# One copy of V, overwritten in place, and eight probability buffers in the first attention of a two-layer block

## The reference

```python
H, D = 16, 64
q = (x @ Wq).reshape(B, S, H, D).transpose(0, 2, 1, 3)
k = (c @ Wk).reshape(B, N, D, H).transpose(0, 3, 2, 1)
v = (c @ Wv).reshape(B, N, D, H).transpose(0, 3, 1, 2)
mask = jnp.all(c == 0, axis=-1)[:, None, None, :]
scores = jnp.einsum('bhsd,bhdn->bhsn', q, k) * scale
att = jax.nn.softmax(jnp.where(mask, -jnp.inf, scores), axis=-1)
out = jnp.einsum('bhsn,bhnd->bhsd', att, v)
x = x + out.transpose(0, 2, 1, 3).reshape(B, S, H * D) @ Wo
```

## Time and profile before

| what | value |
|---|---|
| median of 3 runs | 2121.53 us (2121.21 to 2129.98) |
| the profiled execution | 2127.05 us |
| its span, first to last instruction | 2125.3 us |
| PE, DVE, ACT, POOL busy | 1982.3, 1693.7, 1065.4, 1161.7 us |
| `subtract` L741 | 832 times, 685 ns |
| row maximum L682 | 1024 times, 589 ns |
| copy of a V chunk by ACT L556 | 208 times, 592 ns |
| denominator sum on POOL L374 | 352 and 32 times, 2.4 us |

### The profile page before, as it was taken

One profiled execution on the slowest core, in us unless ns is written; L12 is line 12 of the kernel. 1 busy time (PEld: TensorE's weight loads), 2 busy tenths in 40 slices (PEclk: granted clock), 3 DMA queues, 4 the chain that ended last, 5 costly groups with the idle time before them and its releaser, 6 DMA issues. The chain is left out here.

```text
span 2125.3 us, 35171 instructions
## 1 busy us (share of the span) xinstructions
PE 1982.3 (93%) x10757; PEld 1451.8 (68%) x10757; DVE 1693.7 (80%) x4048; ACT 1065.4 (50%) x1493; POOL 1161.7 (55%) x624
## 2 busy tenths in 40 slices
PE   5999999999999999999999999999966899779995
PEld 4677777777677777767777777777645688557774
DVE  7898888888887888888888888888647777757765
ACT  3445445453545545453545545454534799644442
POOL 0275756657575655757575666657764445314340
PEclk9899999999999999999999999999986999879997
DMA  3000000000000000000000000000000212112210
GB/s 95 1 1 17 1 4 17 1 1 4 18 1 4 2 16 1 4 18 1 1 4 17 1 4 1 1 1 1 1 6 16 91 60 75 38 49 63 74 35 24
DMA packets 54855, 40.84 MB, mean 19 GB/s; under 512 B 2500, under 2 KB 51596, under 8 KB 53644
## 3 DMA queue, kind: packets, MB, share of 16 engines
q1 hardware_dynamic: 54668, 38.57, 6.1%
HBM read 37.45 MB, written 1.11 MB: 18 GB/s over the span
## 5 line engine op out<-in xcount | busy, mean ns | idle before, releaser
L374 POOL TENSOR_TENSOR a_den<-a_den,a_probs 128x1024 f32<-128x1024 f32 x352 | 844.3, 2402 | 332.2 <-ACT a_probs L572 331.8
L572 ACT ACTIVATE a_probs<-a_probs,a_mask_col 128x1024 f32<-128x1024 f32 x416 | 478.8, 1151 | 571.8 <-DVE a_probs L741 571.7
L741 DVE TENSOR_TENSOR a_probs<-a_scores,a_shift 128x512 f32<-128x512 f32 x832 | 565.0, 685 | 160.1 <-PE a_scores L399 138.8
L682 DVE CUSTOM_DVE_ANT_0 a_work<-a_work,a_mask_row 128x400 f32<-128x400 f32 (+1 forms) x1024 | 571.7, 589 | 47.7 <-PE a_work L431 47.3
L479 PE MATMUL a_pv<-a_probs,a_V 128*64 128x256 f32 x3328 | 405.2, 385 | 1.0 <-ACT a_probs L572 0.9
L397 PE MATMUL a_scores<-a_Q_hi,a_cT_hi 128*128 128x512 f32 x832 | 345.7, 415 | 6.4 <-DVE a_probs L741 4.6
L431 PE MATMUL a_work<-a_cT_hi,a_Q_hi 128*128 128x400 f32 (+1 forms) x1024 | 328.0, 369 | 2.4
L398 PE MATMUL a_scores<-a_Q_lo,a_cT_hi 128*128 128x512 f32 x832 | 328.1, 394 | 0.0
L399 PE MATMUL a_scores<-a_Q_hi,a_cT_lo 128*128 128x512 f32 x832 | 326.6, 393 | 0.0
L479 PEld LDWEIGHTS a_pv<-a_probs,a_V 128*64 128x64 f32 x3328 | 220.5, 136 | 150.3 <-issue 39.1
L431 PEld LDWEIGHTS a_work<-a_cT_hi,a_Q_hi 128*128 128x128 f32 x1024 | 193.7, 190 | 98.3 <-issue 43.1
(11 more groups left out here) (319 smaller groups left out, 2849.4 us busy)
## 6 DMA issues: line engine op xcount, KB each, us to landing
m_gate_rows<-gate_scratch SPq DMA_DIRECT2D x8, 1024.0 KB, 4.9
a_c_nat<-in_ctx_dram SPq DMA_DIRECT2D x8, 768.0 KB
b_c_in<-in_ctx_dram SPq DMA_DIRECT2D x8, 768.0 KB
b_c_nat<-in_ctx_dram SPq DMA_DIRECT2D x8, 768.0 KB
m_w_raw<-in_L_ffn_W_dram SPq DMA_DIRECT2D x16, 256.0 KB, 5.0
a_acc<-in_x_dram SPq DMA_DIRECT2D x8, 128.0 KB, 2.1
out_dram<-tokens SPq DMA_DIRECT2D x4, 256.0 KB, 2.3
a_V<-in_L_xattn_Wq_dram SPq DMA_DIRECT2D x1, 512.0 KB, 6.6
```

The costliest lines, as they stand in the source:

```text
L374: nc.gpsimd.tensor_tensor(half, so_far, probs[:, buffer(c, j), :], ALU.add).then_inc(den_added, 1)
L572: nc.scalar.activation(probs[:, buffer(c, j), :], probs[:, buffer(c, j), :], ACT.Exp, bias=mask_col[:, c // 2 % 2, j // 2:j // 2 + 1]).the ...
L682: nc.vector.tensor_tensor_reduce(out=X[:, bank, :w], in0=X[:, bank, :w], in1=mask_row[:, off:off + w], scale=1.0, scalar=-3e38, op0=ALU.ad ...
L741: nc.vector.tensor_tensor(probs[:, buffer(c, j), pair * 2 * S:(pair + 1) * 2 * S], Sc[:, pair, :], shift[:, first:first + 2 * S], ALU.add) ...
```

## The change

`V` has one copy. A chunk of the next stage's V is now projected in the odd step that last reads this chunk, right behind its PV (`v_slot`: slots 6, 15, 22, 31, up to 102, one chunk in every eight slots). ACT's copy of it waits for that PV. `V_AFTER` and `LATE_V` go, and the row maxima close up in slots 0 to 91. `probs` has eight buffers, and the subtraction waits for the step eight back. `group_ends` and `group_of` put PV's order in general terms; with `GROUP = 2` it is the same as before. The raw weights of the setup now lie in the only copy of V.

```diff
-    V_AFTER = [1, 4, 6, 8, 10, 12, 14, 26, 38]
-    LATE_V = [95, 97, 100, 102]
+    BUFFERS = 8
+    GROUP = 2
+
+    def group_ends(j):
+
+        return j % GROUP == GROUP - 1 or j == STEPS - 1
+
+    def group_of(j):
+
+        return range(j - j % GROUP, j + 1)
+
+    def v_slot(chunk):
+
+        end = next(j for j in range(2 * chunk + 1, STEPS) if group_ends(j))
+        return 4 * end + 2 + chunk % 2
...
-        vs = [("v", c) for c in range(NC)]
-        for u in range(UNITS * 4):
-            early.append(("max", u))
-            if u in V_AFTER:
-                early.append(vs.pop(0))
+        early += [("max", u) for u in range(UNITS * 4)]
...
-        assert len(vs) == len(LATE_V)
-        for n, item in zip(LATE_V, vs):
-            slots[n].append(item)
+        for chunk in range(NC):
+            slots[v_slot(chunk)].append(("v", chunk))
...
-        V = sb("V", [P, 2, NC, G8 * HD])
+        V = sb("V", [P, NC, G8 * HD])
...
-        probs = sb("probs", [P, 4, 4 * S])
+        probs = sb("probs", [P, BUFFERS, 4 * S])
...
-            return (c * STEPS + j) % 4
+            return (c * STEPS + j) % BUFFERS
...
-                        if part == 1 and j % 2 == 1:
-
-                            for both in (j - 1, j):
-                                pv(it, c, both, 0)
-                                pv(it, c, both, 1)
+                        if part == 1 and group_ends(j):
+
+                            for step in group_of(j):
+                                pv(it, c, step, 0)
+                                pv(it, c, step, 1)
...
-                    nc.scalar.activation(V[:, s % 2, i, :], X[:, bank, :], ACT.Copy).then_inc(bank_free[bank], 1)
+                    if c >= 0:
+
+                        act.wait_ge(pv_done, steps_of(it, c, 2 * i + 2))
+                    nc.scalar.activation(V[:, i, :], X[:, bank, :], ACT.Copy).then_inc(bank_free[bank], 1)
...
-                    if c > 0 or j > 3:
-
-                        dve.wait_ge(pv_done, steps_of(it, c, j - 3))
-                        added = 1 if j == 4 else 2 if j == 5 else j - 5 if j > 5 else j - 3
+                    if c > 0 or j >= BUFFERS:
+
+                        last = j - BUFFERS
+                        dve.wait_ge(pv_done, steps_of(it, c, last + 1))
+                        added = last + 1 if last in (0, 1) or last < 0 else last - 1
```

More of the change, by code:

```diff
@@ L227, in attention_0 @@
         ones_r = sb("ones_r", [P, P], F32R)
-        raw = [V[:, 1, :, :].rearrange("p c n -> p (c n)")[:, i * 1024:(i + 1) * 1024] for i in range(6)]
+        raw = [V[:, :, :].rearrange("p c n -> p (c n)")[:, i * 1024:(i + 1) * 1024] for i in range(6)]
         wq_raw, wk_raw, wv_raw, wk_heads, wqT, wkT = raw
@@ L479, in pv @@
                     last = nc.tensor.matmul(PV[HD * odd:HD * odd + HD, cols:cols + S],
-                                            V[:, c % 2, j // 2, h * HD:(h + 1) * HD],
+                                            V[:, j // 2, h * HD:(h + 1) * HD],
                                             probs[:, buffer(c, j), (pair * 2 + odd) * S:(pair * 2 + odd + 1) * S],
```

## The result

| | median | runs | ratio to before, 95% interval |
|---|---|---|---|
| before | 2123.48 us | 4 | |
| after | 2147.73 us (2142.28 to 2149.37) | 4 | 1.0105 (1.0074 to 1.0135) |

The account below looks back on a forecast made before the run. DVE was taken to bound slots 10 to 25 and PE the rest; 7 x (1.4 even + 1.0 odd) - 1 before the first stage = +15.8 us on the median 2121.53, forecast 2137.3 us, range 2116 to 2148.

Parts of the forecast that it names:

- W2 and W3: Slots 10 to 25, beside the reciprocals: DVE sets the pace, more maxima cost +1.18 us (even), +1.1 (odd stages).
- W6 to W11: Six windows at PE's pace: more chunks, fewer maxima, +2.18 us, less 0.6 of PE's waits, per stage.
- W1: Slots 2 to 9: no change; in odd stages a query item is swapped for a chunk of the same columns.
- W4 + W5: A stage's fourth and fifth windows, at PE's pace: 0 in even stages, -0.32 us in odd ones.
- W12 and the next W0: Slots 90 to 103 and the next stage's 0 and 1: one chunk fewer in each window, -1.36 us a stage.
- the query's low part: Odd stages, slots 10 to 25: one more query item there costs DVE 0.60 us, priced as a subtraction.
- Before the first stage and in stage 0: Chunks 9 and 10 leave the spread matmuls and chunk 11 fills a gap: about -1 us; stage 0 unchanged.
- the first rival: Even spreading pays for itself: PE loses nearly all removable waits, 1.9 us instead of 0.6; 2119 us, chance 0.22.
- The buffers: Eight probability buffers remove a stage's first subtraction's wait for POOL's sum, priced at nothing, bounds 0 and 13.0 us.
- The second (buffers): Rival: that first subtraction's wait reaches PE, so 13.0 us less and chunks cost nothing; 2108.5 us, chance 0.08.
- the third (V copies hold PE's banks): Rival: PE waits for banks until ACT's V copies finish, 25 us more, 2162 us; chance 0.10 together with the fourth.
- the fourth (ACT held by its new wait): Rival: the added wait holds ACT, so exponentials come late and PV waits; chance 0.10 together with the third.

Follow-up runs that it names:

- e1: The changed kernel with four probability buffers in place of eight: 2146.09 us, 1.0083 of before.
- e2: The kernel before with only the V chunks in their new places (two copies of V, four buffers, no added wait): 2147.09 us, 1.0085 of before.
- e3: The kernel before with each reciprocal over 2 of its 128 columns: 2110.34 us, 0.9915 of before.
- e6: e5 with the odd stages' masks and queries also moved forward: 2122.56 us, 0.9976 of before.
- e10: The kernel before with a reciprocal in every third slot instead of every second, normalisation and projection moved behind them: 2114.32 us, 0.9941 of before.
- e11: The changed kernel with a reciprocal in every third slot instead of every second, normalisation and projection moved behind them: 2138.89 us, 1.006 of before.
- e9: e6 with a reciprocal in every third slot, normalisation and projection moved behind, and row maxima set between the reciprocals: 2115.74 us, 0.9946 of before.
- e4: The changed kernel with each reciprocal over 2 of its 128 columns: 2106.9 us, 0.9904 of before.
- e5: The changed kernel with row maxima taken out of slots 10 to 25, all but two (even) or three (odd stages): 2129.4 us, 1.0016 of before.
- e12: The changed kernel with PV behind every step in place of every second: 2192.88 us, 1.0326 of before.

## Why the prediction was right, and where its terms were off

The mechanism held: the loss is in W2 and W3, by DVE's load. That the time lies inside the range is in part luck: it is above the 2146 that the forecast gave as its own bound (no gain in W6 to W11), and two of the four runs, 2148.77 and 2149.37, lie outside the range. By the medians the change cost 24.3 us, by the profiled executions 21.7, where 15.8 was forecast. The window means over the seven stages of each kind, against the terms of the sum (us a stage):

| term | even: forecast | even: measured | odd: forecast | odd: measured |
|---|---|---|---|---|
| W1 | 0 | -0.10 | 0 | +0.25 |
| W2 + W3 | +1.18 | +1.06 | +1.1 | +2.04 |
| W4 + W5 | 0 | -0.13 | -0.32 | -1.32 |
| W6 to W11 | +1.58 | +0.99 | +1.58 | +1.54 |
| W12 and the next W0 | -1.36 | -0.47 | -1.36 | -0.72 |
| sum | +1.4 | +1.35 | +1.0 | +1.79 |

**Even stages.** The sum held, and so did the step that carried it: DVE's three maxima more in W2 and W3 at 0.5 us each, less its idle time. The last two rows were each off and in opposite directions, because work that a window ends with or takes over shifts between neighbours; together they were forecast at +0.22 and came to +0.52. PE's waits in W12 rose by 0.33 us (0.24 to 0.57), which the prediction had at none. No run looked for the cause.

**Odd stages.** Here the sum was 0.8 us a stage too low, 5.5 us over seven, and this is what the total was off by: 7 x (1.35 + 1.79) = 22.0 against 7 x (1.4 + 1.0) = 16.8. W2 and W3 grew by 0.9 us more than the maximum and the query's low part, and W4 and W5 fell by 1.0 more, so windows alone do not place the miss. PE's waits do it better. The forecast had them at +1.6 in W2 and W3 (1.1 more time and 0.5 less work: two chunks less, a max and a query more) and -0.6 in W6 to W11; measured are +1.86 and -0.49, and +0.29 in W1 and +0.20 in W12, where I had none. So the miss has several parts.

Most of W1's part is one stage of the profiled execution. In stage 9 W1 took 10.09 us, in the other odd stages 8.4 to 8.5, and the granted clock of TensorE was lower in it, so that part of it ran at the lower level, 1.2 GHz. The first line is the stretch ahead of it, where PE was idle for 1.9 us, the last is stage 3's W1:

```profile
940.00:948.42 8.42, 6.51 (x39) 4.54 (x38) 4.43 (x8) 4.42 (x8) 0.31 (x1) 1.00 0.02 7
948.42:958.51 10.09, 9.63 (x52) 5.80 (x51) 7.79 (x17) 4.41 (x8) 2.55 (x2) 0.83 0.29 84
...
366.57:375.05 8.48, 8.48 (x55) 5.96 (x55) 7.60 (x17) 4.42 (x8) 3.44 (x2) 1.00 0.35 97
```

These 1.6 us are 0.23 of the 0.25 by which the mean of W1 grew. The same W1, longer by 1.1 to 1.6 us, stands in stage 5 or 9, where the loop begins its second and third turn, in the profiled executions of e1, e2, e3, e6, e10 and e11, in both stages of e9, and in none of before, e4 and e5. The granted clock was lower each time. It comes with kernels on both sides of the change (e3 and e10 are before with other reciprocals), so it is not put down to the change; why the clock fell was not looked for. Without it the odd sum is 0.56 us a stage too low, not 0.8. In the table of waits such a stage makes about 0.2 us in the odd columns W1 and whole stage.

The step that I had wrong is the price of the query item that moved into W2: I took its own instruction on DVE and left out the chain in front of it, ACT's exponential and copy, for which DVE stands 0.84 us. This is nearly all of the 0.9 us by which W2 and W3 were longer than forecast, but W4 and W5 give as much back, and in PE's waits W2 and W3 are only 0.26 us above the forecast. e6 moves the queries, and PE's waits in an odd stage fall by 0.63 us (9.41 to 8.78), by 0.86 without the one W1, but the maxima are moved away in it too. What the chain alone costs in after stays open, and so does W12, as in the even stages.

**Before the first stage and in stage 0.** The first subtraction came at 78.53 us, 1.6 before its former 80.12 (forecast: 1). Stages 0 and 15 together took 0.8 more, and the part behind the first attention 0.6.

**The waits of W6 to W11.** The forecast took 0.6 us off, since DVE has three maxima fewer there. PE's waits there fell by 0.92 us in even and 0.49 in odd stages. That the even ones gave more than 0.6 fits their single windows: W7, for one, had seven maxima and no chunk, and DVE was all but full in it, which the sum over six windows, 35.17 of 38.49, hid:

```profile
316.32:322.67 6.35, 6.35 (x37) 4.41 (x36) 6.22 (x19) 2.31 (x3) 4.77 (x2) 1.00 0.01 3
```

This was the term that decided between the forecast and the first rival, which needed over 1.7.

**The buffers.** Nothing, as priced; after and e1, eight and four of them in the new places, do not differ. But the prediction misread the wait of the earlier trace rows. Its row is gone from the lists of e1 and e2, which have four buffers, so it was the places that took it away. And it had hardly been a wait for POOL: a wait for several things is put down to the one that came last, and the subtraction's own scores had come just before. In before the last score matmul of this subtraction starts at 353.65, and the subtraction at 354.25:

```profile
353.65 0.39 PE L399 MATMUL a_scores<-a_Q_hi,a_cT_lo 128*128 128x512 f32 x1
```

In after the two start at 356.26 and 356.87, and the list puts the wait down to the scores. PE's score group behind it starts right behind PV, as it did in the earlier trace rows:

```profile
356.26 0.40 PE L407 MATMUL a_scores<-a_Q_hi,a_cT_lo 128*128 128x512 f32 x1
356.87 1.43 DVE L753 TENSOR_TENSOR a_probs<-a_scores,a_shift 128x512 f32<-128x512 f32 x2 [0.64 <-PE a_scores L407]
...
357.73 1.95 PE L487 MATMUL a_pv<-a_probs,a_V 128*64 128x256 f32 x16
359.61 0.51 PE L405 MATMUL a_scores<-a_Q_hi,a_cT_hi 128*128 128x512 f32 x1
```

The subtraction starts 0.6 us behind its last score matmul with the wait for POOL as without it, and so it does in all twelve stages of the earlier trace rows.

By the Trainium skill (Perfetto Trace Analysis, Optimization Strategy) a gap that keeps coming back on the engine that should be saturated can mean too few buffers. For the 13.0 us of such gaps the traces do not bear it out: with eight buffers the subtraction came no sooner behind its scores, and PE's score group, which starts behind PV, was the later one anyway.

**The rivals.** The first (even spreading pays) fell with the waits above. The second (buffers) fell with the starts above; as a run of before with eight buffers it was not tried. For the third (V copies hold PE's banks) the list of waits of after has one wait of PE for ACT's copy of a V chunk, 0.5 us. For the fourth (ACT held by its new wait) ACT's copies of V wait for their own matmuls only, 338.4 us in all, and none is put down to PV; e2, which has no such wait, is as slow.

The same section of the Trainium skill says that a kernel with several regimes, where the engine that is contended changes, can gain from interleaving them. This describes the kernel before better than I had read it: its V chunks, work of PE and ACT alone, stood beside DVE's reciprocals. The change took them apart for a layout that looks even, and by the table PE's waits in W2 and W3 rose by 2 us a stage. e10 goes one step further beside the reciprocals, and in odd stages it took 0.9 us of waits out of W2 and W3.

## What to carry to other kernels

Even by count is not even by load: where two engines are both near full, lay out each one's work so that every short stretch (here two steps, about 7 us) balances by itself, and put work that one engine does alone next to the other's heaviest. An engine that is free on the average over a stage does not help PE if its work comes in lumps that stand ahead of what PE waits for, and this shows only in windows. Before adding buffers, look whether the one that waits is late for somebody, and whether the row of the list names what held it: compare its start with that of its other inputs.

## What the runs showed of the hardware that was not expected

- A switch of PE from score and max matmuls to PV and back cost 0.2 us by the starts in e12, and 0.19 to 0.27 by PE's waits; 26 PV groups a stage in place of 13 cost 2.1% of the time (from 2147.73 to 2192.88 us). Whether it is PV's width, 64 in place of 128, was not tested.
- The busy share of PE stayed at 93% while the kernel became 1% slower. In W2 and W3 of an even stage of after PE is idle for 1.05 us by its busy time (15.73 of 16.78) and waits 3.51 by its starts: the rest hides between records that overlap.
- One stage of a profiled execution at a lower granted clock (0.83 over 10.09 us) cost 1.6 us. It came and went between executions, and in means over seven stages it looked like an effect of the change.
